# Splitting one write into three and regrouping the operand loads of a fused gate and attention kernel

## The chip, the cores and the metric

The kernel runs on one core of a Trainium2 chip. Five engines work from queues of their own and meet at semaphores: TensorE (PE; its weight loads are shown as PEld), VectorE (DVE), ScalarE (ACT), GpSimd (POOL) and SyncE (SP), which here only issues DMAs. The metric is the device time of one execution in microseconds.

## The reference

The input x is 32 images of 64 channels by 16 x 16 pixels. A first layer gates it by channel and by place; a second is a group norm followed by attention with 4 heads over the 256 pixels of an image. Cut to what matters here:

```python
yc = sigmoid(x * conv1d(mean(x))[:, :, None, None])
x1 = yc * sigmoid(conv2d([mean_c(yc), max_c(yc)])) + x
q, k, v = split(qkv_w @ groupnorm(x1) + qkv_b)          # 4 heads of 16 channels
attn = softmax(einsum('bndi,bndj->bnij', q, k) * 0.25)  # 256 x 256 per head
out = x1 + proj_w @ einsum('bnij,bndj->bndi', attn, v) + proj_b
```

## The kernel before, in words

**Tiling.** Two images stand on the 128 partitions and form a pair; there are 16 pairs. The attention is done per unit, which is one head of one image: 8 units a pair, numbered 0 to 7.

**Scores from split operands.** q and k are needed closer than bfloat16 holds them. Each is split into three bfloat16 parts, 0 (coarse) to 2 (fine), whose sum is the float32 value. Six products of parts are kept. So each operand of a score matmul has 6 x 16 = 96 rows: `qs` and `ks` hold, slot by slot, the parts of q and of k whose products are wanted. A 97th row holds the negated row maxima in `qs` and ones in `ks`, which the transposed scores need.

**How the operands get there.** ScalarE evicts q and k in bfloat16 as part 0 (line 414) and again in float32 (line 417); GpSimd makes the rest (333), part 1 (345) and part 2 (347). The tile `parts` is written to DRAM by one DMA on SP's queue (263, tensor `parts_dram`), and six DMAs (256 and 257) load it back, with the repetitions that the 96 rows ask for. The row of maxima goes through a DMA of its own (244, from `maxrow` to `qs`), issued ahead of those loads. `parts_dram`, `qs`, `ks` and `parts` have a ring of 4 slots for the pairs.

**The order of work.** The order on every engine is written out by hand. `pipeline` calls a function `turn(k, ...)` for turns k = -5 to 17; turns 3 to 10 are a hardware loop of two laps of four. In turn k pair k+1 has its scores (line 667) and maxima (546), pair k and k-1 their transposed scores (679) and exponentials (408): units 4 to 7 of pair k-1 in the first half and 0 to 3 of pair k in the second. The transposed scores of unit 0, at u = 4, wait for `mrow_in`, the landed row of maxima of pair k. Pair k+2 has its operands loaded, pair k+3 is split and written, pair k-3 is added up and stored (271). The first score matmul of a turn waits for `stack_in`, all loads of its pair. `slot(d)` is the ring slot of pair k+d, `has(d)` says whether that pair exists. SP's queue issues in its written order and holds what stands behind a wait. Two reads of gates (212) stand at the end of SP's turns 0 and 1, one more of them is on ScalarE's queue.

The profile counts the packets that the core's 16 DMA engines move, and their busy time as a share of those 16.

Of the kernel before, what the change touches and what calls it, by code (L numbers as in the profile page):

```python
# [24 lines left out]
N = SIDE * SIDE  # L25
PAIRS = IMAGES // 2
HEADS, HD = 4, 16
# [7 lines left out]
RING = 4  # L35
# [17 lines left out]
def program(nc, x, w_rows, vecs, w_all, select, consts, out):  # L53
    ctx = ExitStack()
    with ctx:
# [3 lines left out]
        def sem(name):  # L59
            return ctx.enter_context(nc.semaphore(name))  # L60
# [94 lines left out]
        z_ready, v_ready = sem("z_ready"), sem("v_ready")  # L155
        p1_ready, z32_ready = sem("p1_ready"), sem("z32_ready")
        split_step = sem("split_step")
        parts_out, stack_in = sem("parts_out"), [sem(f"stack_in{r}") for r in range(RING)]
        s_ready, max_done = sem("s_ready"), sem("max_done")
        mt_ready, mrow_ready, mrow_in = sem("mt_ready"), sem("mrow_ready"), sem("mrow_in")  # L160
        st_ready, exp_done = sem("st_ready"), sem("exp_done")
# [56 lines left out]
        @block.sync  # L218
        def _(sp):
            sp.dma_start(wrow[:, :], w_rows.partition_broadcast(P)).then_inc(rows_in, 16)  # L220
            sp.dma_start(con[:, 0:C_IDENT], consts[:, 0:C_IDENT]).then_inc(con_in, 16)
            for g in range(GROUPS):
                sp.dma_start(xall[:, g * GROUP:(g + 1) * GROUP, :],
                             x[2 * g * GROUP:2 * (g + 1) * GROUP].rearrange("(g i) c n -> (i c) g n", i=2)).then_inc(x_in[g], 16)
                if g == 0:
                    sp.dma_start(sel[:, :], select).then_inc(sel_in, 16)
                    sp.dma_start(con[:, C_IDENT:C_END], consts[:, C_IDENT:C_END]).then_inc(ident_in, 16)

            sp.wait_ge(toep_zero, 1)
            sp.wait_ge(band_ready, 2)  # L230
            for y in range(SIDE // TILES):
                r = slice(SIDE * y, SIDE * (y + 1))
                dst = toep[r, :].rearrange("p (a c) -> p a c", c=TSTRIDE)[:, :, y * SIDE:(y + KS) * SIDE]
                sp.dma_start(dst, bandrow[r, :, :, :].rearrange("p t m n -> p (t m) n")).then_inc(toep_in, 16)
            sp.dma_start(wall[:, :], w_all).then_inc(wall_in, 16)
            sp.dma_start(vec[:, :], vecs).then_inc(vec_in, 16)
            gate_write(sp, 0, 0, 2 * GROUP)
            gate_read(sp, 0)
            aside = {(0, 2): lambda: gate_read(sp, 2), (1, 2): lambda: gate_read(sp, 3)}

            def turn(k, slot, has, lap):
                if has(0):
                    wait(sp, mrow_ready, k + 1)
                    sp.dma_start(qs[KQ:KQ + 1, slot(0), :, :, :].rearrange("p h a (t n) -> p (h a t) n", t=TILES),  # L244
                                 maxrow[:, slot(0), :]).then_inc(mrow_in, 16)


                if has(2):
                    r = slot(2)
                    wait(sp, parts_out, 16 * (k + 3))  # L250
                    for first, q_parts, k_part in ((0, 3, 0), (3, 2, 1), (5, 1, 2)):

                        rows = slice(first * HD, (first + q_parts) * HD)
                        src_q = parts_dram[r, 0:q_parts, 0, :, :].rearrange("s d n -> d s n")
                        src_k = parts_dram[r, k_part, 1, :, :].unsqueeze(1).broadcast_to([HD, q_parts, HEADS * 2 * N])
                        sp.dma_start(qs[rows, r, :, :, :].rearrange("p h a n -> p (h a n)"), src_q).then_inc(stack_in[r], 16)  # L256
                        sp.dma_start(ks[rows, r, :, :, :].rearrange("p h a n -> p (h a n)"), src_k).then_inc(stack_in[r], 16)  # L257


                if has(3):  # L260
                    r = slot(3)
                    wait(sp, split_step, 3 * (k + 4))
                    sp.dma_start(parts_dram[r].rearrange("s g d (h n) -> (g d h) s n", h=HEADS), parts[:, r, :, :]).then_inc(parts_out, 16)

                if has(-3):
                    wait(sp, out_ready, k - 2)
                    if isinstance(k, int):
                        dst = out[2 * (k - 3):2 * (k - 2)].rearrange("i c n -> (i c) n")
                    else:
                        dst = out[bass.ds(2 * (k - 3), 2)].rearrange("i c n -> (i c) n")  # L270
                    sp.dma_start(dst, at(xall, k - 3)).then_inc(stored, 16)
                stands_in(aside, k, 2)
            pipeline(sp, turn)
            sp.wait_ge(out_ready, PAIRS)
            sp.dma_start(out[2 * (PAIRS - 1):2 * PAIRS].rearrange("i c n -> (i c) n"), xall[:, PAIRS - 1, :]).then_inc(stored, 16)
            sp.wait_ge(stored, 16 * PAIRS)
# [3 lines left out]
        def _(pool):  # L280
# [21 lines left out]
            def turn(k, slot, has, lap):  # L302

                if has(-3):
                    wait(pool, yo_ready, k - 2)
                    nc.gpsimd.tensor_tensor(at(xall, k - 3), yo[:, slot(-3), :], at(xall, k - 3), ALU.add).then_inc(out_ready, 1)  # L306

                if has(5) and not (isinstance(k, int) and k + 5 in EARLY):
                    if isinstance(k, int) and k + 4 in EARLY:
                        pool.wait_ge(x1_ready, k + 5)  # L310
                    for g in [(k + 5) // GROUP] if isinstance(k, int) else range(1, GROUPS):
                        pool.wait_ge(gate_in[g], 32)
                    nc.gpsimd.tensor_tensor(at(ycall, k + 5), at(ycall, k + 5), at(gate, k + 5), ALU.mult).then_inc(u_ready, 1)
                    pool.wait_ge(u_ready, k + 6)
                    nc.gpsimd.tensor_tensor(at(xall, k + 5), at(ycall, k + 5), at(xall, k + 5), ALU.add).then_inc(x1_ready, 1)

                if has(4):
                    wait(pool, gn_var, k + 5)
                    nc.gpsimd.tensor_tensor(sq[:, :], gmv[:, 2:3], gmv[:, 2:3], ALU.mult).then_inc(sq_ready, 1)
                    nc.gpsimd.tensor_tensor(posvar[:, :], eps[:, :], gmv[:, 1:2], ALU.subtract).then_inc(posvar_ready, 1)  # L320
                    wait(pool, sq_ready, k + 5)
                    wait(pool, posvar_ready, k + 5)
                    nc.gpsimd.tensor_tensor(vareps[:, :], sq[:, :], posvar[:, :], ALU.add).then_inc(vareps_ready, 1)
                    wait(pool, vareps_ready, k + 5)
                    nc.gpsimd.tensor_tensor(rstd[:, :], vareps[:, :], mhalf[:, :], ALU.pow).then_inc(rstd_ready, 1)

                on_pool = has(3) and not (isinstance(k, int) and k + 3 == 0)
                if on_pool:
                    r = slot(3)
                    wait(pool, p1_ready, k + 4)  # L330
                    wait(pool, z32_ready, k + 4)
                    wait(pool, split_step, 3 * (k + 3))
                    nc.gpsimd.tensor_tensor(rest[:, :], z32[:, :], parts[:, r, 0, :], ALU.subtract).then_inc(split_step, 1)  # L333
                    wait(pool, split_step, 3 * (k + 3) + 1)

                if has(4):
                    wait(pool, rstd_ready, k + 5)
                    wait(pool, xn_ready, k + 4)
                    nc.gpsimd.tensor_tensor(gna[:, :], rstd[:, :], w_gn, ALU.mult).then_inc(gn_scale, 1)
                    wait(pool, gn_scale, k + 5)  # L340
                    nc.gpsimd.tensor_tensor(gnm[:, :], gmv[:, 0:1], gna[:, :], ALU.mult).then_inc(gn_mean, 1)
                    wait(pool, gn_mean, k + 5)
                    nc.gpsimd.tensor_tensor(gnb[:, :], gnm[:, :], b_gn, ALU.add).then_inc(gn_shift, 1)  # L343
                if on_pool:
                    nc.gpsimd.tensor_scalar(parts[:, r, 1, :], rest[:, :], 1.0, 0.0, ALU.mult, ALU.add).then_inc(split_step, 1)
                    wait(pool, split_step, 3 * (k + 3) + 2)
                    nc.gpsimd.tensor_tensor(parts[:, r, 2, :], rest[:, :], parts[:, r, 1, :], ALU.subtract).then_inc(split_step, 1)  # L347
            pipeline(pool, turn)
# [3 lines left out]
        def _(act):  # L352
# [37 lines left out]
            def turn(k, slot, has, lap):  # L390
                for u in range(UNITS):
# [18 lines left out]

                    if u == 0 and has(3):
                        wait(act, z_ready, k + 4)
                        wait(act, parts_out, 16 * k)
                        nc.scalar.activation(parts[:, slot(3), 0, :], z_bank[:, :], ACT.Identity, bias=b_qk).then_inc(p1_ready, 1)  # L414
                    if u == 1 and has(3):
                        wait(act, split_step, 3 * (k + 2) + 1)
# [162 lines left out]
        def _(pe):  # L579
# [79 lines left out]
            def turn(k, slot, has, lap):  # L659
                def s(u):  # L660
# [1 line left out]
                    a, h = u // HEADS, u % HEADS  # L662
                    wait(pe, max_done, UNITS * (k + 1) + u - 1)
                    if u == 0:
                        wait(pe, stack_in[slot(1)], lap(1) * 96)
                    for t in range(TILES):
                        mm = pe.matmul(s_bank[u % 2][:, t * N:(t + 1) * N], qs[0:KQ, slot(1), h, a, t * P:(t + 1) * P],  # L667
                                       ks[0:KQ, slot(1), h, a, :], start=True, stop=True)
# [156 lines left out]
```

## Time and profile before

| | |
|---|---|
| median of 3 runs (lowest to highest) | 199.0 us (196.49 to 199.06) |
| the profiled execution: its time, its span | 195.77 us, 193.9 us |
| granted TensorE clock, mean over the span | 0.982 |
| busy: TensorE, VectorE, ScalarE, GpSimd | 168.6, 142.1, 122.6, 112.2 us |
| DMA | 26.24 MB, mean 135 GB/s; queue q1 holds 16 engines busy for 51.1% of the span |
| chain that ended last | PE 34%, DMA 23%, SP's queue 20%, DVE 7% |

A share of the span is a mean over stages of different kinds. The main loop lies between some 40 and 178 us; ahead of it the gates are computed, behind it the last pairs are finished. The chain follows the last instruction back through what released each step, so a large share of DMA and SP's queue in it says that in part of the turns TensorE waited for a load.

### The profile page before, as it was taken

What the parts mean: (1) busy time and instruction counts of PE and PEld (TensorE: products, weight loads), DVE (VectorE), ACT (ScalarE), POOL (GpSimd) and SP (SyncE); (2) the same over time, 40 slices, a digit from 0 to 9 for tenths busy, and PEclk for the clock granted to TensorE, in tenths of its full rate; (3) what the DMA queues carried; (4) which work ended last, traced back from release to release, by engine and by line L of the source; (5) the groups of instructions that cost most, each with busy time, mean ns of one, the idle gap of its engine ahead of it and who ended that gap; (6) DMA issues with size and microseconds to landing.
All of it is one profiled execution on the core that took longest, in us unless ns stands there. A gap on an engine that the chain in (4) does not pass through costs nothing.

```text
span 193.9 us, 4752 instructions
## 1 busy us (share of the span) xinstructions
PE 168.6 (87%) x1515; PEld 105.4 (54%) x1518; DVE 142.1 (73%) x295; ACT 122.6 (63%) x250; POOL 112.2 (58%) x214
## 2 busy tenths in 40 slices
PE   7698985986959999989999998999999898888881
PEld 2265674453546667565656666576666655453320
DVE  0947769256743998888989897897989679797353
ACT  3073540451537797968878696977879686657760
POOL 5991282858473948678686968679784370101110
PEclk9969999999996999999999999999999999999999
DMA  3940302779397684637485755736676574600011
GB/s 100 358 111 19 108 3 83 167 221 210 84 227 163 165 202 122 158 119 167 148 172 144 194 126 145 162 124 148 194 177 129 154 163 125 176 28 3 28 32 54
DMA packets 19558, 26.24 MB, mean 135 GB/s; under 512 B 3756, under 2 KB 16468, under 8 KB 19540
## 3 DMA queue, kind: packets, MB, share of 16 engines
q1 hardware_dynamic: 18960, 25.47, 51.1%
q10 hardware_dynamic: 580, 0.55, 1.1%
q8 instruction: 10, 0.16, 0.4%
q14 instruction: 8, 0.07, 0.1%
HBM read 17.35 MB, written 8.42 MB: 133 GB/s over the span
## 4 chain that ended last, share of the span: by engine, by line
PE 34%; DMA 23%; SPq 20%; DVE 7%; POOL 6%; ACT 5%; issue 5%; POOLq 0%; ACTq 0%
DMA ks<-parts_dram 18%; SPq L256 11%; PE bank L667 7%; PE bank L693 7%; SPq L257 6%; PE bank L679 5%; PE bank L703 3%; DMA parts_dram<-parts 3%; PE bank L606 3%; DVE negmax L546 2%; SPq L244 2%; ACT pt L408 2%; PE bank L722 2%; DMA con<-consts 2%; PE bank L713 1%
## 5 line engine op out<-in xcount | busy, mean ns | idle before, releaser
L546 DVE TENSOR_REDUCE negmax<-bank 128x2 bf16<-128x512 f32 x128 | 86.1, 683 | 27.4 <-PE bank L667 24.9
L408 ACT ACTIVATE pt<-bank 128x512 f32<-128x512 f32 x128 | 73.5, 592 | 19.1 <-PE bank L679 18.9
L667 PE MATMUL bank<-ks,qs 96*128 96x256 bf16 x256 | 49.9, 276 | 11.3 <-DMA ks<-parts_dram 8.9
L679 PE MATMUL bank<-qs,ks 97*128 97x256 bf16 x256 | 49.2, 274 | 2.1 <-ACT pt L408 2.0
L667 PEld LDWEIGHTS bank<-ks,qs 96*128 96x128 bf16 x256 | 20.5, 101 | 38.5 <-DVE negmax L546 23.6
L693 PE MATMUL bank<-pt,vs 128*32 128x256 f32 x512 | 34.0, 383 | 0.1
L333 POOL TENSOR_TENSOR rest<-z,parts 128x512 f32<-128x512 f32 x15 | 17.4, 1158 | 27.5 <-ACT z L417 14.8
L679 PEld LDWEIGHTS bank<-qs,ks 97*128 97x128 bf16 x256 | 24.3, 98 | 8.2 <-ACT pt L408 4.6
L306 POOL TENSOR_TENSOR xall<-yo,xall 128x256 f32 (+1 forms) x15 | 10.9, 726 | 26.0 <-ACT yo L428 25.9
L693 PEld LDWEIGHTS bank<-pt,vs 128*32 128x32 f32 x512 | 14.8, 110 | 12.3 <-issue 3.4
L703 PE MATMUL bank<-xn,wall 128*128 128x256 f32 x64 | 20.0, 400 | 1.0 <-ACT xn L400 0.9
L583 PE MATMUL bank<-warm 128*128 128x512 bf16 x57 | 19.4, 455 | 1.7 <-POOL warm L283 1.4
L347 POOL TENSOR_TENSOR parts<-rest,parts 128x512 bf16<-128x512 f32 x15 | 17.4, 1161 | 1.2
L414 ACT ACTIVATE parts<-bank,vec 128x512 bf16<-128x512 f32 x16 | 10.8, 677 | 9.2 <-PE bank L703 9.1
L519 DVE STREAM_TRANSPOSE otok<-bank 128x512 f32<-128x512 f32 (+1 forms) x17 | 11.5, 676 | 5.2 <-PE bank L693 5.2
L396 ACT COPY maxrow<-bank 16x128 bf16<-16x128 bf16 x16 | 4.1, 255 | 16.9 <-PE bank L744 16.9
L400 ACT ACTIVATE xn<-xall,gnb,gna 128x256 f32<-128x256 f32 (+1 forms) x16 | 9.6, 600 | 7.3 <-POOL gnb L343 7.1
L722 PE MATMUL bank<-onorm,wall 128*32 128x256 f32 x128 | 10.2, 391 | 1.6 <-DVE onorm L530 1.6
L530 DVE STREAM_TRANSPOSE onorm<-otok 128x512 f32<-128x512 f32 (+1 forms) x17 | 11.4, 672 | 0.1
L417 ACT ACTIVATE z<-bank,vec 128x512 f32<-128x512 f32 x16 | 11.0, 685 | 0.0
L583 PEld LDWEIGHTS bank<-warm 128*128 128x128 bf16 x60 | 6.7, 119 | 7.6 <-issue 4.3
L703 PEld LDWEIGHTS bank<-xn,wall 128*128 128x128 f32 x64 | 9.8, 190 | 1.6 <-ACT xn L400 1.0
(70 smaller groups left out, 216.1 us busy)
## 6 DMA issues: line engine op xcount, KB each, us to landing
parts_dram<-parts SPq DMA_DIRECT2D x16, 384.0 KB, 2.6
qs<-parts_dram SPq DMA_DIRECT2D x16, 192.0 KB, 3.7
ks<-parts_dram SPq DMA_DIRECT2D x16, 192.0 KB, 4.0
xall<-x SPq DMA_DIRECT2D x4, 512.0 KB, 5.9
qs<-parts_dram SPq DMA_DIRECT2D x16, 128.0 KB, 3.9
ks<-parts_dram SPq DMA_DIRECT2D x16, 128.0 KB, 3.8
out<-xall SPq DMA_DIRECT2D x16, 128.0 KB, 2.2
gate<-gate_dram SPq DMA_DIRECT2D x6, 256.0 KB, 4.1
```

The costliest lines, as they stand in the source:

```text
L256: sp.dma_start(qs[rows, r, :, :, :].rearrange("p h a n -> p (h a n)"), src_q).then_inc(stack_in[r], 16)
L257: sp.dma_start(ks[rows, r, :, :, :].rearrange("p h a n -> p (h a n)"), src_k).then_inc(stack_in[r], 16)
L333: nc.gpsimd.tensor_tensor(rest[:, :], z32[:, :], parts[:, r, 0, :], ALU.subtract).then_inc(split_step, 1)
L347: nc.gpsimd.tensor_tensor(parts[:, r, 2, :], rest[:, :], parts[:, r, 1, :], ALU.subtract).then_inc(split_step, 1)
L408: nc.scalar.activation(pt[:, (u + LEAD) % UNITS, :, :].rearrange("p t n -> p (t n)"), st_bank[u % 2][:, :], ACT.Exp, scale=SCALE).then_inc ...
L546: nc.vector.tensor_reduce(negmax[:, slot(1), column:column + TILES], s_bank[u % 2][:, :].rearrange("p (t n) -> p t n", t=TILES), AX.X, ALU ...
L583: pe.matmul(bank[:, :], warm[:, 0:P], warm[:, :], start=True, stop=True)
L667: mm = pe.matmul(s_bank[u % 2][:, t * N:(t + 1) * N], qs[0:KQ, slot(1), h, a, t * P:(t + 1) * P], ks[0:KQ, slot(1), h, a, :], start=True, ...
L679: mm = pe.matmul(st_bank[u % 2][:, t * N:(t + 1) * N], ks[0:KQ + 1, slot(d), h, a, t * P:(t + 1) * P], qs[0:KQ + 1, slot(d), h, a, :], sta ...
L693: mm = pe.matmul(o_bank[32 * h:32 * h + 32, a * N:(a + 1) * N], vs[:, slot(-1), t, a, h, :], pt[:, HEADS * a + h, t, :], start=(t == 0), s ...
L703: mm = pe.matmul(z_bank[:, a * N:(a + 1) * N], w_qk[a], xn[:, slot(d), :], start=True, stop=True)
L722: mm = pe.matmul(y_psum[C * a + j:C * a + j + 32, :], w_p[:, j:j + 32], onorm[:, a * N:(a + 1) * N], start=True, stop=True)
```

## The change

The one write of `parts` becomes three, one for each part, each with a semaphore of its own: part 0 as soon as ScalarE has made it, the output's store, then part 1 and part 2. The slots of `qs` and `ks` are assigned anew, so that each load needs one part alone: q has part 0 in slots 0 to 2, part 1 in 3 and 4, part 2 in 5; k has part 0 in slots 1, 4 and 5, part 1 in 2 and 3, part 2 in 0. The same six products of parts are formed. That makes seven loads of one part in 1, 2 or 3 copies instead of six. The three loads of part 0 stand ahead of the row of maxima on SP's queue, the other four behind it. GpSimd waits, ahead of making part 2, for the transposed scores of pair k-1, whose slots the early loads reuse. The source of a load is written `[copies, 16, ...]` now; it was `[16, copies, ...]` or `[16, parts, ...]`.

```diff
-        parts_out, stack_in = sem("parts_out"), [sem(f"stack_in{r}") for r in range(RING)]
+        parts_out, stack_in = [sem(f"parts_out{i}") for i in range(3)], [sem(f"stack_in{r}") for r in range(RING)]
...
             def turn(k, slot, has, lap):
+                def stack(tile, g, part, first, copies):
+                    r = slot(2)
+                    rows = slice(first * HD, (first + copies) * HD)
+                    src = parts_dram[r, part, g, :, :].unsqueeze(0).broadcast_to([copies, HD, HEADS * 2 * N])
+                    sp.dma_start(tile[rows, r, :, :, :].rearrange("p h a n -> p (h a n)"), src).then_inc(stack_in[r], 16)
+
+                def part_write(part):
+                    r = slot(3)
+                    sp.dma_start(parts_dram[r, part].rearrange("g d (h n) -> (g d h) n", h=HEADS),
+                                 parts[:, r, part, :]).then_inc(parts_out[part], 16)
+
+                if has(2):
+                    wait(sp, parts_out[0], 16 * (k + 3))
+                    stack(qs, 0, 0, 0, 3)
+                    stack(ks, 1, 0, 1, 1)
+                    stack(ks, 1, 0, 4, 2)
                 if has(0):
                     wait(sp, mrow_ready, k + 1)
                     sp.dma_start(qs[KQ:KQ + 1, slot(0), :, :, :].rearrange("p h a (t n) -> p (h a t) n", t=TILES),
                                  maxrow[:, slot(0), :]).then_inc(mrow_in, 16)
                 if has(2):
-                    r = slot(2)
-                    wait(sp, parts_out, 16 * (k + 3))
-                    for first, q_parts, k_part in ((0, 3, 0), (3, 2, 1), (5, 1, 2)):
-                        rows = slice(first * HD, (first + q_parts) * HD)
-                        src_q = parts_dram[r, 0:q_parts, 0, :, :].rearrange("s d n -> d s n")
-                        src_k = parts_dram[r, k_part, 1, :, :].unsqueeze(1).broadcast_to([HD, q_parts, HEADS * 2 * N])
-                        sp.dma_start(qs[rows, ...], src_q).then_inc(stack_in[r], 16)
-                        sp.dma_start(ks[rows, ...], src_k).then_inc(stack_in[r], 16)
+                    wait(sp, parts_out[1], 16 * (k + 3))
+                    stack(qs, 0, 1, 3, 2)
+                    stack(ks, 1, 1, 2, 2)
+                    wait(sp, parts_out[2], 16 * (k + 3))
+                    stack(qs, 0, 2, 5, 1)
+                    stack(ks, 1, 2, 0, 1)
                 if has(3):
-                    r = slot(3)
-                    wait(sp, split_step, 3 * (k + 4))
-                    sp.dma_start(parts_dram[r].rearrange("s g d (h n) -> (g d h) s n", h=HEADS), parts[:, r, :, :]).then_inc(parts_out, 16)
+                    wait(sp, p1_ready, k + 4)
+                    part_write(0)
                 if has(-3):
                     wait(sp, out_ready, k - 2)
...
+                if has(3):
+                    wait(sp, split_step, 3 * (k + 3) + 2)
+                    part_write(1)
+                    wait(sp, split_step, 3 * (k + 4))
+                    part_write(2)
...
                     nc.gpsimd.tensor_scalar(parts[:, r, 1, :], rest[:, :], 1.0, 0.0, ALU.mult, ALU.add).then_inc(split_step, 1)
+                    wait(pool, st_ready, UNITS * k)
                     wait(pool, split_step, 3 * (k + 3) + 2)
...
-                        wait(act, parts_out, 16 * k)
+                        wait(act, parts_out[0], 16 * k)
...
-                        wait(pe, stack_in[slot(1)], lap(1) * 96)
+                        wait(pe, stack_in[slot(1)], lap(1) * 112)
```

## Rows read from the trace of the kernel before

**Rows 1.** Stretches: window, length, busy us per engine (instructions), granted clock, DMA share, GB/s.

```profile
101.80:110.40 8.60, 8.28 (x85) 5.39 (x85) 7.41 (x16) 6.88 (x14) 6.52 (x13) 1.00 0.61 150
...
104.20:104.40 0.20, 0.20 (x5) 0.16 (x8) 0.20 (x2) 0.20 (x2) 0.00 (x0) 1.00 0.00 0
104.40:109.20 4.80, 4.67 (x61) 2.74 (x54) 3.84 (x8) 3.99 (x9) 3.77 (x7) 1.00 0.78 167
105.40:105.60 0.20, 0.20 (x4) 0.17 (x3) 0.05 (x1) 0.20 (x1) 0.20 (x1) 1.00 1.14 389
...
58.00:62.00 4.00, 4.00 (x25) 2.69 (x26) 2.06 (x3) 2.98 (x6) 0.77 (x1) 0.57 0.63 160
```

**Rows 2.** Timeline of TensorE: start us, length us, what, idle before and its releaser.

```profile
39.96 0.39 PE L667 MATMUL bank<-ks,qs 96*128 96x256 bf16 x2 [0.84 <-DMA ks<-parts_dram]
...
101.81 0.38 PE L667 MATMUL bank<-ks,qs 96*128 96x256 bf16 x2 [0.33 <-DMA ks<-parts_dram]
...
105.88 0.38 PE L679 MATMUL bank<-qs,ks 97*128 97x256 bf16 x2
...
127.69 0.38 PE L667 MATMUL bank<-ks,qs 96*128 96x256 bf16 x2
...
135.96 0.38 PE L667 MATMUL bank<-ks,qs 96*128 96x256 bf16 x2
...
161.60 0.38 PE L667 MATMUL bank<-ks,qs 96*128 96x256 bf16 x2 [0.88 <-DMA ks<-parts_dram]
...
170.02 0.38 PE L667 MATMUL bank<-ks,qs 96*128 96x256 bf16 x2 [1.13 <-DMA ks<-parts_dram]
```

**Rows 3.** Timeline of SP's queue: start us, length us, DMA issued.

```profile
30.72 0.39 SPq L263 DMA_DIRECT2D parts_dram<-parts  x1
...
102.78 0.55 SPq L244 DMA_DIRECT2D qs<-maxrow  x1
103.45 0.56 SPq L256 DMA_DIRECT2D qs<-parts_dram  x1
...
107.24 0.42 SPq L257 DMA_DIRECT2D ks<-parts_dram  x1
108.94 0.38 SPq L263 DMA_DIRECT2D parts_dram<-parts  x1
...
111.39 0.53 SPq L244 DMA_DIRECT2D qs<-maxrow  x1
```

**Rows 4.** The load of line 257 issued at 107.24: time from issue to landing.

```profile
DMA to landing us min/median/max: 3.1/3.1/3.1
```

**Rows 5.** Timeline of ScalarE and GpSimd in the same turn.

```profile
103.15 0.67 ACT L414 ACTIVATE parts<-bank,vec 128x512 bf16<-128x512 f32 x1
...
107.75 1.16 POOL L347 TENSOR_TENSOR parts<-rest,parts 128x512 bf16<-128x512 f32 x1
```

**Rows 6.** The page's DMA queues: packets, MB, share of 16 engines.

```profile
q1 hardware_dynamic: 18960, 25.47, 51.1%
q10 hardware_dynamic: 580, 0.55, 1.1%
```

**Rows 7.** DMA issues of the whole execution: count, KB each, median us to landing.

```profile
parts_dram<-parts SPq DMA_DIRECT2D x16, 384.0 KB, 2.6
qs<-parts_dram SPq DMA_DIRECT2D x16, 192.0 KB, 3.7
...
gate<-gate_dram ACTq DMA_DIRECT2D x2, 256.0 KB, 3.9
qs<-maxrow SPq DMA_DIRECT2D x16, 4.0 KB, 1.7
...
gate_dram<-gate_s ACTq DMA_DIRECT2D x1, 24.0 KB
```

More of the change, by code:

```diff
@@ L248, in turn @@
                 if has(2):
-                    r = slot(2)
-                    wait(sp, parts_out, 16 * (k + 3))
-                    for first, q_parts, k_part in ((0, 3, 0), (3, 2, 1), (5, 1, 2)):
-                        rows = slice(first * HD, (first + q_parts) * HD)
-                        src_q = parts_dram[r, 0:q_parts, 0, :, :].rearrange("s d n -> d s n")
-                        src_k = parts_dram[r, k_part, 1, :, :].unsqueeze(1).broadcast_to([HD, q_parts, HEADS * 2 * N])
-                        sp.dma_start(qs[rows, r, :, :, :].rearrange("p h a n -> p (h a n)"), src_q).then_inc(stack_in[r], 16)
-                        sp.dma_start(ks[rows, r, :, :, :].rearrange("p h a n -> p (h a n)"), src_k).then_inc(stack_in[r], 16)
+                    wait(sp, parts_out[1], 16 * (k + 3))
[4 more added lines that the diff above has]
+                    stack(ks, 1, 2, 0, 1)
                 if has(3):
-                    r = slot(3)
-                    wait(sp, split_step, 3 * (k + 4))
-                    sp.dma_start(parts_dram[r].rearrange("s g d (h n) -> (g d h) s n", h=HEADS), parts[:, r, :, :]).then_inc(parts_out, 16)
+                    wait(sp, p1_ready, k + 4)
+                    part_write(0)
                 if has(-3):
```

## The prediction

> **What bounds the kernel now.** I read first the busy time by turn. In a turn of the main loop TensorE is busy 8.28 of 8.60 us [rows 1], so the kernel is close to a TensorE bound, and what is left to win is the distance between that and the turn as it runs. The starts of the first score matmul of a turn (line 667, unit 0) show it [rows 2]: an undisturbed turn, from 127.69 to 135.96, lasts 8.27 us; the fifteen turns from 39.96 to 170.02 have a mean of (170.02 - 39.96) / 15 = 8.67 us. Where the two differ, the row names the load of the key operand as the releaser: 0.33 us of idle at 101.81, 0.88 us at 161.60, 1.13 us at 170.02. The SP queue shows where that load comes from [rows 3]: the row of maxima goes out at 102.78, the first of six loads at 103.45, the last at 107.24, and it lands 3.1 us later [rows 4], at 110.34; the next turn's row of maxima follows at 111.39. That is a loop through SP's queue, about as long as TensorE's own turn. The work that the loads bring is 192 packets of 4 KB a turn (96 rows for each operand), carried by 16 DMA engines.
>
> **What the change means to do.** Three of the loads need only part 0, which ScalarE makes at 103.15 [rows 5], 4.6 us before GpSimd begins part 2 at 107.75. Written alone, part 0 is in DRAM early, and its loads can be issued in the gap between the write at 108.94 and the row of maxima at 111.39 [rows 3]. Behind the row of maxima four loads remain instead of six: two issues less (103.45 to 107.24 is five steps of 0.76 us on average, one of them slow; a load's own row shows 0.56), so the last operand lands at least 1.1 us earlier. That covers every idle in rows 2. If this were all, turns would fall to 8.27 us: 15 x (8.67 - 8.27) = 6.0 us, and about 0.8 us each for the first load and for the last two turns, which have less TensorE work: some 8 us.
>
> **The small parts.** SP issues one load more (0.6 us) and two writes more (0.38 us each, the length of the write's row): 1.4 us. Writes 0 and 1 and the store fall into the time in which SP waits for part 2 now (107.66 to 108.94), so the three loads have 109.32 to 111.39 for their 1.9 us. Nothing lost as long as that gap is there; without it the row of maxima would go out up to 1.9 us later. GpSimd's new wait, ahead of the subtraction at 107.75, is for the transposed scores of unit 3; the ones of unit 4 start at 105.88 [rows 2], so it is over 1.8 us before it is reached; behind it are only that subtraction and the next turn's additions. ScalarE's wait is for a write of four pairs ago. The store of the output now goes between write 0 and write 1 and waits for nothing, as before. The row of maxima now stands behind three loads; that is a rival below. TensorE's wait counts seven loads instead of six.
>
> **The term that decides: on how many DMA engines a load runs.** The new loads are written in another order of dimensions. Before, the source of a load was [16 rows, copies, 4 KB] and the copies lay inside; `stack` puts the copies outside, [copies, 16 rows, 4 KB], with 3 or 2 copies in four of the seven loads. The trace shows that a transfer isn't always carried by all 16 engines, if one counts packets [rows 6]. On queue q10 there are three transfers: two gate reads (64 x 4 rows of 1 KB, so 256 packets each) and one store of 24 rows [rows 7]. 512 + 24 are data, and 580 were counted: I read the other 44 as the small packets with which each engine closes its share of a transfer. 16 + 16 leave 12 for the store of 24 rows. Queue q1 comes out to the packet in the same way: by the shapes of its transfers 16,272 data packets (6,144 parts written, 3,072 loaded, 2,048 x, 2,048 out, 1,536 gates, 1,424 the rest), and 167 transfers with a leading count that 16 divides and two of 8 rows: 167 x 16 + 2 x 8 = 2,688, together the 18,960 of the row. So 24 rows used 12 engines, 8 rows 8, and all others 16: the largest number up to 16 that divides the leading count. Read for both sides of a transfer, a leading count of 3 copies gives 3 engines, of 2 copies 2. What no row shows is that the source's leading count alone can narrow a load whose destination has 48 rows, and that narrow loads share the same first engines; I take both: the first because a split into shares must be made on both sides, the second because the simplest way to use fewer than 16 is from the front ((c) below is the other case).
> The Trainium skill states exactly this in "DMA: Bandwidth & Descriptors", section "Why a DMA increments its semaphore by 16 and not by 1": the engines are the largest number up to 16 dividing the slowest dimension of both sides, and a HWDGE transfer takes the lowest-numbered ones; its section "Rules for kernel authors" names "a leading zero-stride broadcast of c copies" as confining the whole DMA to at most c engines. The trace's 580 packets agree with the divisor; no row here shows the choice of the lowest.
>
> **What that costs.** The four wide-copy loads put 16 packets each on engines 0 and 1, the three single ones one packet each: 4 x 16 + 3 = 67 packets on the busiest engine, where before it had 12. One 4 KB packet: in the fastest fifth of a microsecond of a load stage 389 GB/s moved over 16 engines [rows 1], 24.3 GB/s each, 0.168 us; over the whole stage 167 GB/s at a busy share of 0.78 is 13.4 GB/s per busy engine, 0.306 us. With two or three engines asking, the contention of sixteen is gone, so I stay near the fast end and add a little for the first packet of each load: 0.19 us.
> The turn then is a serial loop. Count from the end of the last load's packets. Write 0 of the next pair stands behind them on the same engines; it lands about 0.9 us later (a write of 384 KB lands 2.6 us after issue [rows 7], 1.0 before its first byte, some 1.2 of data, so 0.4 after, and its own packets). Only then does SP pass its wait and issue the loads of part 0; the first byte moves 0.95 us after issue (103.45 issued, nothing moving until 104.40 [rows 1, 3]). 67 packets follow; the row of maxima and the loads of parts 1 and 2 are issued under the first 33, and writes 1 and 2 ran before. Turn = 0.9 + 0.95 + 67 x 0.19 = 14.6 us. Under it TensorE's 8.3 us are hidden: the row of maxima lands about 7.6 us into the turn instead of 2.7, and the half turn that waits for it (8.3 - 4.1 = 4.2 us) ends near 12. Even at the half clock that followed an idle before (0.57 granted over 58 to 62 us [rows 1], 1.2 GHz in most of it) it ends near the 14.6, not far beyond.
> The sum: write 2 of pair 0 goes out at 30.72 as before [rows 3], its loads start at about 31.1 and move from 32.1; 67 x 0.19 = 12.7, and 1.1 to land (107.24 + 3.1 against data that ends by 109.2), so the first scores start at 45.9 instead of 39.96. Fifteen turns of 14.6 are 219: 264.9. After 170.02 the kernel has 193.9 - 170.02 = 23.9 us without loads, unchanged: 288.8. Three gate reads of 512 KB pass over the same engines, about 1 us each: 292. Outside the span lie 195.8 - 193.9 = 1.9 us: 294. This stands against the profiled execution's 195.8; the median of the runs is 199.0, so I say 296. With 0.168 us a packet: 13.2 a turn, 271. With 0.306: 22.4 a turn, 419. If the 1.85 us of latency were half hidden, the fast end would be 257.
>
> **The rivals.**
> (a) *Every load still runs on 16 engines* (the copies are moved inside when the transfer is made, or the destination's 48 rows decide). For it: no transfer of this kernel has unequal leading counts, so rows don't exclude it. Against: a count of 24 was not rounded up to 16 engines. Time: 195.8 - 8 = 188. This is the one on the other side, and it decides as soon as the closing packets of a load are 16.
> (b) *16 engines, and the row of maxima is late.* It now follows three loads on every engine. At 102.78 it needed 1.7 us [rows 7] and the fifth transposed score (105.88) needs it 3.1 us after issue. Behind a load issued 0.6 us ahead, that lands 3.7 us after its own issue [rows 7], it lands 3.2 to 3.7 us after issue: 0.1 to 0.6 us late, half of it given back since a longer turn leaves more room. Turns of 8.4 to 8.6: 191 to 195, no measurable change.
> (c) *Narrow, but each load on other engines.* Then a load takes 16 packets, about 3 us, at its own place; the last ones land in time, and the row of maxima lands 5.6 us into the turn instead of the 4.1 wanted: 0.8 us a turn after the give-back, 9.1 x 15 - 8.67 x 15 = 6: 202.
>
> **Chances.** Forecast 0.82, (a) 0.09, (b) 0.04, (c) 0.05. A run can tell about 2 per cent, 4 us. Faster 0.09; same 0.06, from (b) and half of (c); slower 0.85. The range leaves out the rivals (0.18) and so must hold the bounds of the packet's duration: 255 to 420.
>
> **What would show it.** Packets on q1: 32 more writes close with 512; the loads close with 3 + 2 + 2 + 2 + 3 x 16 = 57 per turn instead of 96, 624 fewer: 18,848. With 16 engines everywhere it would be 18,960 + 512 + 256 = 19,728. The loads of 3 and 2 copies should land 5 us or more after issue, those of part 1 over 8; the mean busy share of the DMA engines should fall under 0.4 while engine 0 is always busy; TensorE should idle twice a turn, before unit 0 on a load and before unit 4's transposed scores on the row of maxima, and its clock should be low in places; the chain should be mostly DMA. If instead loads land in 3 to 4 us, the step on the engines was wrong. If they are narrow and the turn is not near 14.6, the duration of a packet was.

## The result and the profile after

The changed kernel takes 298.5 us (median of 4 runs, 296.75 to 301.34); the kernel before took 198.05 us beside it. The ratio is 1.505, 95% interval 1.488 to 1.522. Forecast were 296 us, with a range of 255 to 420.

The sharpest prediction was the packet count, 18,848 on q1 if four of the seven loads run on 3, 2, 2 and 2 engines, 19,728 if all run on 16. The page's DMA queues after (packets, MB, share of 16 engines; against [rows 6]):

```profile
q1 hardware_dynamic: 18848, 25.47, 27.9%
q10 hardware_dynamic: 580, 0.55, 0.8%
```

It is the smaller number, to the packet. The bytes are those of before; the share of the 16 engines has fallen from 51.1% to 27.9% of a longer span. The page's DMA issues after (count, KB each, median us to landing; against [rows 7]):

```profile
parts_dram<-parts SPq DMA_DIRECT2D x48, 128.0 KB, 8.9
...
qs<-parts_dram SPq DMA_DIRECT2D x16, 192.0 KB
...
qs<-maxrow SPq DMA_DIRECT2D x16, 4.0 KB, 7.3
```

Two things are to be seen. A write of 128 KB takes 8.9 us to land where one of 384 KB took 2.6, and the row of maxima 7.3 instead of 1.7. And the load has no landing time at all. In the profile of before only the transfers of 8 and of 24 rows lacked one, [rows 7] last line: in these profiles a missing landing time marks a transfer that doesn't run on 16 engines.

The page's chain that ended last, by engine and by line (its first entries), shows what the turns wait for:

```profile
DMA 51%; PE 20%; SPq 16%; DVE 6%; issue 3%; ACT 2%; POOL 1%; POOLq 0%; ACTq 0%
```

Its largest single item is the landing of the writes of `parts`, 38% of the span.

Two consecutive turns by stretches (window, length, busy us per engine with instructions, granted clock, DMA share, GB/s), and a stretch in which only narrow loads are left; against [rows 1]:

```profile
152.60:167.00 14.40, 9.94 (x85) 6.48 (x85) 7.76 (x15) 7.20 (x14) 6.96 (x15) 0.88 0.30 93
167.00:184.40 17.40, 11.53 (x85) 7.01 (x86) 7.44 (x15) 6.99 (x14) 7.02 (x14) 0.68 0.26 77
...
176.50:181.50 5.00, 4.38 (x32) 1.92 (x33) 0.69 (x1) 2.04 (x4) 1.17 (x2) 0.50 0.13 51
```

From 176.5 to 181.5 the DMA share is 0.13, which is 2 of 16 engines, and they move 51 GB/s: 25 GB/s each, 0.16 us for 4 KB. Three 2-copy loads of this pair have been issued by 171.1 us, and yet two engines are busy and not four or six. So the narrow loads do share the same engines, one behind the other. How the turn runs is in SP's queue:

```profile
154.74 0.57 SPq L261 DMA_DIRECT2D qs<-maxrow  x1
...
157.69 0.34 SPq L251 DMA_DIRECT2D parts_dram<-parts  x1
...
167.17 0.74 SPq L247 DMA_DIRECT2D qs<-parts_dram  x1
...
169.19 0.57 SPq L261 DMA_DIRECT2D qs<-maxrow  x1
...
182.61 0.72 SPq L247 DMA_DIRECT2D qs<-parts_dram  x1
```

Write 0, issued at 157.69, lands 9.5 us later, and in that instant (167.17) SP issues the next pair's first load. The row of maxima of 169.19 takes this long, in the view of its line:

```profile
DMA to landing us min/median/max: 7.9/7.9/7.9
```

TensorE in the same stretch (first scores of a turn at 152.60, 167.01 and 184.44; the transposed scores that wait for the row of maxima, at u = 4, at 161.22 and 177.12):

```profile
152.60 0.40 PE L681 MATMUL bank<-ks,qs 96*128 96x256 bf16 x2 [1.26 <-DMA ks<-parts_dram]
...
161.22 0.39 PE L693 MATMUL bank<-qs,ks 97*128 97x256 bf16 x2 [2.73 <-DMA qs<-maxrow]
...
167.01 0.39 PE L681 MATMUL bank<-ks,qs 96*128 96x256 bf16 x2 [1.74 <-DMA ks<-parts_dram]
...
177.12 0.61 PE L693 MATMUL bank<-qs,ks 97*128 97x256 bf16 x2 [5.87 <-DMA qs<-maxrow]
...
184.44 0.64 PE L681 MATMUL bank<-ks,qs 96*128 96x256 bf16 x2
```

The two places where it idles are those that were forecast, but not both in every turn: it waits for the row of maxima in 14 turns of 16 (54.2 us in all), and for the load in 7 (18.3 us, 6.6 of them before the first turn). After the 5.87 us of idle it runs at the granted clock 0.50 (1.2 GHz), and the half turn from 177.12 to 184.44 takes 7.3 us instead of 4.2. Here it is the row of maxima and TensorE that end the turn, and the operands are there before they are wanted. TensorE's turns so vary between 12.5 and 17.4 us, while SP issues the first load of a turn every 14.1 to 16.1 us, 15.1 on average: the loads set the pace, and TensorE's start moves to and fro within it.

### The profile page after: what moved, and what is told of

It reads as the page before. It is cut to its first block, busy times and chain, and to the rows that moved or that the text cites. A ratio compares the mean times of both kernels' runs of the same rounds, so it can differ in the third digit from the quotient of the medians.

```text
span 297.3 us, 4824 instructions
## 1 busy us (share of the span) xinstructions
PE 209.7 (71%) x1515; PEld 126.1 (42%) x1518; DVE 145.0 (49%) x295; ACT 125.1 (42%) x250; POOL 112.8 (38%) x214
## 3 DMA queue, kind: packets, MB, share of 16 engines
q1 hardware_dynamic: 18848, 25.47, 27.9%
## 4 chain that ended last, share of the span: by engine, by line
DMA 51%; PE 20%; SPq 16%; DVE 6%; issue 3%; ACT 2%; POOL 1%; POOLq 0%; ACTq 0%
DMA parts_dram<-parts 38%; SPq L247 14%; DMA qs<-maxrow 12%; PE bank L707 4%; PE bank L693 4%; PE bank L681 3%; PE bank L736 2%; PE bank L717 2%; SPq L261 2%; DVE negmax L560 2%; PE bank L620 2%; DMA con<-consts 1%; ACT pt L422 1%; DVE maps L475 1%; POOL tapprod L306 1%
## 5 line engine op out<-in xcount | busy, mean ns | idle before, releaser
L693 PE MATMUL bank<-qs,ks 97*128 97x256 bf16 x256 | 60.2, 325 | 56.3 <-DMA qs<-maxrow 54.2
L681 PE MATMUL bank<-ks,qs 96*128 96x256 bf16 x256 | 60.4, 325 | 18.7 <-DMA ks<-parts_dram 18.3
L693 PEld LDWEIGHTS bank<-qs,ks 97*128 97x128 bf16 x256 | 27.4, 115 | 70.1 <-DMA qs<-maxrow 35.9
L681 PEld LDWEIGHTS bank<-ks,qs 96*128 96x128 bf16 x256 | 25.8, 117 | 50.4 <-issue 26.7
L707 PE MATMUL bank<-pt,vs 128*32 128x256 f32 x512 | 42.0, 454 | 0.1
L346 POOL TENSOR_TENSOR rest<-z,parts 128x512 f32<-128x512 f32 x15 | 17.4, 1159 | 64.8 <-ACT z L431 28.2
L717 PE MATMUL bank<-xn,wall 128*128 128x256 f32 x64 | 28.3, 541 | 1.0 <-ACT xn L414 0.9
L717 PEld LDWEIGHTS bank<-xn,wall 128*128 128x128 f32 x64 | 14.3, 271 | 2.6 <-ACT xn L414 1.2
L736 PE MATMUL bank<-onorm,wall 128*32 128x256 f32 x128 | 13.6, 509 | 1.6 <-DVE onorm L544 1.6
L727 PE MATMUL bank<-wall,xn 128*128 128x128 f32 x64 | 12.5, 330 | 0.0
L332 POOL TENSOR_TENSOR sq<-gmv 128x1 f32<-128x1 f32 x16 | 3.3, 206 | 23.0 <-DVE gmv L519 23.0
```

Of the source, the lines that this page charges most:

```text
L693: mm = pe.matmul(st_bank[u % 2][:, t * N:(t + 1) * N], ks[0:KQ + 1, slot(d), h, a, t * P:(t + 1) * P], qs[0:KQ + 1, slot(d), h, a, :], sta ...
L707: mm = pe.matmul(o_bank[32 * h:32 * h + 32, a * N:(a + 1) * N], vs[:, slot(-1), t, a, h, :], pt[:, HEADS * a + h, t, :], start=(t == 0), s ...
L717: mm = pe.matmul(z_bank[:, a * N:(a + 1) * N], w_qk[a], xn[:, slot(d), :], start=True, stop=True)
L727: mm = pe.matmul(v_psum[:, t * P:(t + 1) * P], xn[:, slot(1), t * P:(t + 1) * P], w_v, start=True, stop=True)
L736: mm = pe.matmul(y_psum[C * a + j:C * a + j + 32, :], w_p[:, j:j + 32], onorm[:, a * N:(a + 1) * N], start=True, stop=True)
```

## The experiments

Two theories stood against each other. **A**: the loss is the few engines of the loads whose copies stand outermost. **B**: it comes from the split write and from the order on SP's queue. Smaller questions (C to G) are named where they are tried. Ratios are to the kernel before, run on the same chip beside it (196.5 to 198.6 us). The one-copy run, the two that keep some loads narrow, the one with the order turned in the kernel before and the one with write 0 on ScalarE's queue rest on two executions each, which lie within 1.3% of each other. "Wide" below means a load whose outermost count is 16, "narrow" one with 2 or 3 there.

### All of the change but the order of dimensions

The rows of `qs` and `ks` as before, so that every load has 16 rows outermost; three writes, two loads of part 0 early, four behind the row of maxima:

```diff
 if has(2):
     wait(sp, parts_out[0], 16 * (k + 3))
-    stack(qs, 0, 0, 0, 3); stack(ks, 1, 0, 1, 1); stack(ks, 1, 0, 4, 2)
+    stack_k(0, 3, 0); stack_q(5, 1)          # source [16, copies, 4 KB]
 ... row of maxima ...
-    stack(qs, 0, 1, 3, 2); stack(ks, 1, 1, 2, 2)
+    stack_k(3, 2, 1); stack_q(3, 2)          # q: parts 0 and 1
     wait(sp, parts_out[2], 16 * (k + 3))
-    stack(qs, 0, 2, 5, 1); stack(ks, 1, 2, 0, 1)
+    stack_k(5, 1, 2); stack_q(0, 3)          # q: parts 0 to 2
```

> Keeps the three writes, the waits and the early loads, but the row layout and the order of dimensions of the kernel before: k part 0 in three copies and q part 0 in one ahead of the row of maxima, four loads behind it, all with 16 rows outermost. Theory A (the loss is the few engines of the loads whose copies stand outermost): every load closes with 16 packets, q1 counts 18,960 + 512 = 19,472, loads land in 3 to 4 us, turns fall to 8.3 to 8.5 us and the time is 186 to 192 us. Theory B (the loss comes from the split write and the row of maxima behind loads, whatever the order of dimensions): still over 250 us, with the row of maxima landing 5 us or more after issue. Theory C (as A, but the row of maxima, behind two loads, lands too late by some tenths): 192 to 198 us and idle of TensorE ahead of unit 4's transposed scores.

Measured: 188.6 us, ratio 0.965 (0.959 to 0.970). It beats both kernels. Its queue row, one turn by stretches, its waits on DMAs (engine, line, releaser: us in total, times, longest), and its row of maxima:

```profile
q1 hardware_dynamic: 19472, 25.47, 47.6%
```

```profile
103.25:111.50 8.25, 8.12 (x87) 5.47 (x86) 7.28 (x16) 6.94 (x15) 6.53 (x14) 1.00 0.53 161
```

```profile
PE bank L697 <- DMA qs<-maxrow: 2.8, 3, 1.4
...
PE bank L685 <- DMA qs<-parts_dram: 0.8, 2, 0.6
```

```profile
qs<-maxrow SPq DMA_DIRECT2D x16, 4.0 KB, 2.2
```

The turn is 8.25 us with TensorE busy for 8.12 of it, the load waits of [rows 2] are gone, and the row of maxima lands 2.2 us after issue. B has fallen: with the split and early loads in place nothing is lost. C has not come about in the main loop, only in the first three turns (waits of 0.75, 1.45 and 0.59 us up to 67 us), the later two of them beside the gate reads.

### The changed kernel, one copy a load

```diff
+for c in range(first, first + copies):
+    sp.dma_start(tile[c * HD:(c + 1) * HD, r, :, :, :].rearrange("p h a n -> p (h a n)"),
+                 parts_dram[r, part, g, :, :]).then_inc(stack_in[r], 16)
-src = parts_dram[r, part, g, :, :].unsqueeze(0).broadcast_to([copies, HD, HEADS * 2 * N])
```

> The changed kernel with the same rows, bytes and order by part, but each load of 2 or 3 copies issued as 2 or 3 loads of one copy, whose outermost dimension is 16 rows: 12 loads a turn. Theory A: 192 closing packets a turn, so q1 counts 18,848 + 16 x (192 - 57) = 21,008; no narrow load is left and the bound is SP's queue, 12 x 0.6 + 0.55 + 3 x 0.38 + 0.4 = 9.3 us a turn, so 46 - 6 + 15 x 9.4 + 24 + 2 = about 207 us, 200 to 215. Theory B (the split and the order on the queue are what costs): six loads ahead of the row of maxima instead of three make it worse than 298 us.

Measured: 204.8 us, ratio 1.046 (1.038 to 1.054).

```profile
q1 hardware_dynamic: 21008, 25.47, 43.1%
```

```profile
SPq 41%; PE 20%; issue 10%; DMA 9%; DVE 8%; POOL 7%; ACT 3%; POOLq 0%; ACTq 0%
```

The same rows, bytes and order as in the change, five issues more, and 94 us less. The packet count is as expected, and the chain's first entry (second fence, from the page) is SP's queue, 41%. This is the change's own layout without narrow loads, and in this form it doesn't pay: with 12 load issues a turn SP's queue is the longest part of the chain, and TensorE waits 12.7 us in all, in 11 turns, for a row of maxima that lands 1.9 us after its issue but is issued late.

### Only some of the loads narrow

```diff
+if part == 0:      # the mirror run: if part == 1
+    ... one load a copy, as above
+    return
```

> The changed kernel with the loads of part 0 issued copy by copy (6 wide loads), those of part 1 still narrow (2 engines each). The busiest DMA engine carries 6 + 32 + 2 = 40 packets of 4 KB a turn instead of 67. Theory A, serial on the same first engines at the measured 0.16 us each: the turn falls by 27 x 0.16 = 4.3 us, from 15.1 to about 10.8, so 298 - 16 x 4.3 = 229 us, 220 to 240; q1 counts 18,848 + 16 x (96 - 23) = 20,016. The row of maxima is no longer behind narrow loads and lands in under 4.5 us. Theory D (a turn costs what the longest single narrow load costs, loads on separate engines): the last loads are as long as before and the time stays within 5 per cent of 298.

Measured: 256.9 us, ratio 1.312 (1.299 to 1.326); turns of 12.0 us in the main loop. D has fallen, but A's number, 229, is missed too. The packets on q1 are 20,048; the 20,016 expected was a slip (7 loads close with 57 packets, of which part 0 had 3 + 16 + 2 = 21, so 75 x 16 more). SP's queue in a turn says why the turn fell by 3 us only:

```profile
156.26 1.25 SPq L248 DMA_DIRECT2D qs<-parts_dram  x3
157.56 1.34 SPq L248 DMA_DIRECT2D ks<-parts_dram  x3
159.02 0.56 SPq L266 DMA_DIRECT2D qs<-maxrow  x1
159.62 0.64 SPq L252 DMA_DIRECT2D qs<-parts_dram  x1
...
168.19 0.78 SPq L248 DMA_DIRECT2D qs<-parts_dram  x2
```

The first narrow load is issued at 159.62, 3.4 us after write 0 landed: six issues and the row of maxima took the place of the packets that were taken away. I had subtracted packets from a term that is really the longer of packets and issues.

> The mirror of the run with part 0 wide: the loads of part 0 stay narrow (3 and 2 engines), those of part 1 go copy by copy. The busiest engine has 16 + 1 + 16 + 4 + 2 = 39 packets. Theory A: the operands are in time and only the row of maxima is late, since its shares on the first engines stand behind 33 packets. It lands about 0.4 + 2.2 + 6 + 0.5 = 9 us after the write of part 2, which comes 7.1 us into the turn; the half turn behind it needs 4.3 us, so the turn T satisfies T = 16.2 - T + 4.3, 10.3 us, more with a low clock: 225 to 245 us, and TensorE waits on the row of maxima alone. q1 counts 18,848 + 16 x (4 x 16 - 4) = 19,808. Theory D (separate engines, each narrow load only as long as itself): the row of maxima lands under 5 us after issue.

Measured: 250.7 us, ratio 1.279 (1.263 to 1.296), and 19,808 packets on q1. Its waits on DMAs:

```profile
PE bank L698 <- DMA qs<-maxrow: 40.4, 12, 6.9
...
PE bank L686 <- DMA ks<-parts_dram: 4.6, 2, 2.7
```

The place of the loss moved to the row of maxima, nearly alone, as A says. Its landing times alternate: 8.8, 4.3, 8.8 and 4.9 us after issue in the first four turns, 4.9 the median of all. The median alone would meet D's "under 5 us"; the 8.8 us, what A expects behind 33 packets (9 us), do not. The time is a little above the expected 225 to 245.

### The kernel before, with one thing turned

```diff
-src_q = parts_dram[r, 0:q_parts, 0, :, :].rearrange("s d n -> d s n")
-src_k = parts_dram[r, k_part, 1, :, :].unsqueeze(1).broadcast_to([HD, q_parts, HEADS * 2 * N])
+src_q = parts_dram[r, 0:q_parts, 0, :, :]
+src_k = parts_dram[r, k_part, 1, :, :].unsqueeze(0).broadcast_to([q_parts, HD, HEADS * 2 * N])
```

> The kernel before with one thing changed: in its six loads the parts or copies stand outermost on both sides ([3 or 2, 16 rows, 4 KB] instead of [16, 3 or 2, 4 KB]); one write, six loads behind the row of maxima, as before. The order of q's rows within a load turns with it, so its scores pair other rows than the reference's. Theory A: four loads close with 3, 3, 2 and 2 packets, q1 counts 18,960 - 16 x 54 = 18,096; the busiest engine has 66 packets, 10.6 us, and the loop row of maxima, loads, first scores takes 1.0 + 1.2 + 1.0 + 10.6 + 1.1 = 14.9 us: 40 + 6 + 15 x 14.9 + 24 + 2 = 295 us, 280 to 305. Theory B: no split and no early loads, so near 198 us.

Measured: 327.6 us, ratio 1.673 (1.656 to 1.689). (The remark on the pairing was wrong: q's and k's rows turn together, and the same products are formed.)

```profile
q1 hardware_dynamic: 18096, 25.46, 24.5%
```

```profile
PE bank L667 <- DMA ks<-parts_dram: 105.3, 16, 9.0
```

No split, no new load, no new order on the queue: two dimensions changed places, and 131 us are lost against the 196.5 us beside it. TensorE's idle ahead of the scores for the loads went from 8.9 to 105.3 us, and its busy time from 168.6 to 205.0 us as its mean granted clock went from 0.982 to 0.790. A alone is enough. The forecast was again too low, by a tenth: 16.8 us a turn instead of 14.9. The step that was too small is the packet: by the packets' starts in the trace, the loads of a turn take 12.6 us from their first packet to their last, 0.19 us for each of the 66, where 0.16 (10.6 us) was put in; the rest is 4.2 us, as forecast (4.3).

### The loop through write 0

```diff
+# ScalarE, behind the eviction of part 0
+wait(act, p1_ready, k + 4)
+act.dma_start(parts_dram[slot(3), 0]..., parts[:, slot(3), 0, :]).then_inc(parts_out0[slot(3)], 16)
-# SyncE, behind the loads
-part_write(0)
```

> The changed kernel, narrow loads kept, but the write of part 0 issued from ScalarE's queue right behind the eviction instead of behind the loads on SP's queue (a semaphore for each ring slot). Theory A with its loop (the loads of part 0 wait for a write that stands behind the narrow loads on the same engines): the loads of the next pair can be issued while the last ones run, the busiest engines work without a pause, 16 x 0.2 + 51 x 0.16 + 32 x 0.047 = 12.9 us a turn, so the turn falls from 15.1 to 13 to 13.8 and the time to 263 to 280 us. Theory F (the write's landing is not a link; the turn is set by the row of maxima and the half turn after it): 292 to 304 us.

Measured: 268.7 us, ratio 1.372 (1.357 to 1.386). The waits on DMAs:

```profile
PE bank L682 <- DMA ks<-parts_dram: 35.0, 13, 6.9
PE bank L694 <- DMA qs<-maxrow: 19.8, 13, 2.6
```

The mean turn is 12.9 us, as estimated for a busiest engine that works without a pause. In the changed kernel no 4 KB packet moves for 2.4 us in every turn, between the last packet of one pair's loads and the first of the next; here no such break of over 0.8 us is left. So write 0, standing behind the narrow loads, was a link of the loop and cost 2.2 us a turn; F has fallen.

### Where the gain of the wide version comes from

Its early loads moved behind the row of maxima:

> The wide version by part (188.6 us) with its two early loads moved behind the row of maxima: three writes, then six loads behind it as in the kernel before. Theory A for the gain of the wide version (what it wins is two load issues and their data taken off the loop row of maxima, loads, first scores): back to the time before within 1.5 per cent, 193 to 199 us, with TensorE waiting on loads at the start of turns again and turns of 8.5 to 8.9 us. Theory E (the gain is the earlier writes): stays at 187 to 190 us.

```diff
-if has(2): wait(sp, parts_out[0], 16 * (k + 3)); stack_k(0, 3, 0); stack_q(5, 1)
 ... row of maxima ...
+if has(2): wait(sp, parts_out[0], 16 * (k + 3)); stack_k(0, 3, 0); stack_q(5, 1)
```

Measured: 193.9 us, ratio 0.984 (0.971 to 0.997): between the two, at the lower edge of what A expected. TensorE waits for loads again (4.8 us in 5 turns; 8.9 us in 10 in the kernel before). By the ratios some half of the gain needs the early loads (1.9 of 3.5 per cent). The rest may be the split's, but the interval reaches up to 0.997, so that this share is hardly told apart from nothing.

One write of all parts, but the two loads early:

> The kernel before with one write of all parts, but the two loads that need part 0 alone ahead of the row of maxima, all wide. They wait for the landing of the whole write, 2.5 us after part 2 is made, which is when the row of maxima is ready. Theory A: the row of maxima then goes out 1.3 us later and behind 256 KB, lands 5 to 6 us into the turn instead of 2.7 and TensorE waits for it at unit 4: turns of 8.9 to 9.5 us, 200 to 209 us, so the early loads pay only with the write split. Theory G (the early loads alone bring the gain, split or not): 187 to 192 us.

```diff
+if has(2): wait(sp, parts_out, 16 * (k + 3)); stack_k(0, 3, 0); stack_q(5, 1)
 ... row of maxima ...
-    wait(sp, parts_out, 16 * (k + 3)); ... six loads
+    stack_k(3, 2, 1); stack_q(3, 2); stack_k(5, 1, 2); stack_q(0, 3)
```

Measured: 202.4 us, ratio 1.034 (1.029 to 1.039). Its largest wait on a DMA:

```profile
PE bank L690 <- DMA qs<-maxrow: 9.9, 10, 1.7
```

Here SP passes the wait for the one write late, and the row of maxima mostly goes out 2 to 3 us after the turn's first score matmul, where the kernel before has 1.0 (102.78 against 101.81, [rows 2, 3]). The early loads alone don't pay; they need the split, which lets them go in the gap. Last, in turns 1 and 2 of the wide version the row of maxima ahead of the early loads:

> The wide version by part, but in turns 1 and 2, where 512 KB of gates have just been issued on the same queue, the row of maxima goes ahead of the two early loads. In the wide version TensorE waits there 1.45 and 0.59 us for the row of maxima, which lands 4 us after issue. Expected: those waits go, turns 1 and 2 fall from 9.1 and 8.7 us to 8.3 to 8.7, so 186.5 to 188 us, 0.5 to 1 per cent under the wide version; if the operands of these turns come late instead, no change.

```diff
+late = isinstance(k, int) and k in (1, 2)
-if has(2):
+if has(2) and not late:
     part 0 loads
 ... row of maxima ...
+if late: part 0 loads
```

Measured: 187.3 us, ratio 0.955 (0.945 to 0.965). The waits on the row of maxima fall from 2.8 to 1.8 us, but the interval overlaps that of the wide version: no difference is shown.

## Why the prediction was right, point by point

- **Distance to the TensorE bound.** Right: with all loads on 16 engines turns fall to 8.25 us (8.27 read from [rows 2]) and the time to 188.6; rival (a) had said 188.
- **The small parts cost nothing.** Right; the wide version holds all of them but one of the early loads.
- **A load's engines are the largest number up to 16 that divides the leading counts.** Right, in six packet counts: 18,848, 19,472, 21,008, 20,048, 19,808 and 18,096. Both things that no row had shown held: the source's leading count narrows a load of 48 rows, and narrow loads share their engines. The Trainium skill's rule on the lowest-numbered engines ("DMA: Bandwidth & Descriptors", section "Why a DMA increments its semaphore by 16 and not by 1") agrees with the second as far as the share of 0.13 goes; which engines they are, the trace doesn't say.
- **The loop through write 0.** Right: taken out, the turn falls from 15.1 to 12.9 us.
- **The size of the turn, 14.6 us: right, but one term of it by luck.** It was 15.13 on average ((272.65 - 45.74) / 15). By the packets' starts in the trace, 12.8 us pass from the first to the last 4 KB packet of a turn's loads, which is 0.19 us for each of the 67, as forecast. Then no 4 KB packet moves for 2.4 us, until write 0 has landed and the next loads begin; the sum had 0.9 + 0.95 = 1.85. That is the missing half microsecond. But 0.19 was not found where the prediction looked. Its fast end of 0.168 us divided 389 GB/s by 16 engines at a share that the row gives as 1.14; divided by that share too, as was done for the 13.4 GB/s, it would have been 0.19 us. And packets that run alone take 0.16. The slower ones come in the first part of a turn:

```profile
168.70:176.50 7.80, 2.56 (x30) 1.39 (x28) 3.77 (x8) 2.79 (x6) 3.47 (x6) 0.80 0.43 129
176.50:180.30 3.80, 3.17 (x26) 1.59 (x30) 0.69 (x1) 2.04 (x4) 0.00 (x0) 0.50 0.13 52
```

In the second stretch the two engines start 24 packets each, 0.16 us apart. In the first, while single-copy loads, the row of maxima, the writes and the store move too, the slower of the two gets through some 34, 0.23 us each (an estimate: 67 less what it moved later). Whether those packets were slower or stood in pauses isn't shown, since the trace's packets name no engine. That the kernel before with its order turned was forecast too low, with 0.16 us a packet, fits this. (For the case of 0.168 us the sum gives 13.1 us a turn, not the 13.2 written.)

- **TensorE is hidden under the loop.** Half right: true at full clock. At 1.2 GHz the half turn behind the row of maxima takes 7.3 us, and TensorE ends many turns: of the 15 turn starts after the first, 9 show no wait for the load, and one turn lasts 17.4 us. The prediction had allowed for "not far beyond". The mean stays that of the loads.
- **The signs.** The mean DMA share on q1 is 0.28 (under 0.4 forecast) and the chain is mostly DMA. That the loads land late couldn't be read, since they have no landing time. That "engine 0 is always busy" doesn't hold: in every turn 2.4 us pass without a 4 KB packet on any engine.
- **Begin and end.** The first scores start at 45.74 (45.9 forecast); behind the last turn's start lie 24.65 us (23.9).
- **Rival (b)**, the row of maxima late on 16 engines, is not seen in the main loop with two early loads of 256 KB (2.2 us to land). With the change's 384 KB on 16 engines there is only the one-copy run, where it lands 1.9 us after issue but goes out late. **(c)** fell with the share of 0.13: on engines of their own the 2-copy loads would have been over by 176.5.

## What to carry to other kernels

Look at the outermost dimension of both sides of every DMA as it is written: with 2 or 3 copies there, a load ran on 2 or 3 engines here. Put the 16 rows outside and the copies inside; the bytes are the same. In a profile the signs are a landing time that is missing, small closing packets that don't come out to 16 a transfer, and a DMA share of few sixteenths (two, here) while everything waits. And when one link of a loop is made shorter, ask what the next longest of issue, packets and landing is before subtracting.

## What the runs showed of the hardware

- One engine moved 4 KB rows at 25 GB/s when two were at work; sixteen together averaged 13.4 GB/s per busy engine in the stage of [rows 1]. A load on two engines is thus slower by some 16 / 2 x 13.4 / 25 = 4.3 times, and not by 8 (an estimate from the two rates).
- A 4 KB transfer on all 16 engines took 7.9 us to land behind narrow loads, where the median in the kernel before is 1.7.
- With write 0 on ScalarE's queue it took 6.2 us to land (median; 8.9 for all writes in the changed kernel), but the two writes left on SP's queue took 6.3 in that run. That the other queue makes a write land sooner is thus not shown; what it did was to let write 0 go out right behind its eviction, before the last loads of the turn (154.09, where SP issued loads up to 155.5).
- On two engines, 4 KB packets followed each other at 0.16 us while nothing else moved, and took 0.19 on average over the loads of a turn, in the changed kernel and in the kernel before with its order turned.
